# A two-layer graph network on one core: the seven-product form of A g built from four integer block sums on GpSimd and one difference on VectorE

## What is computed

```
deg = max(sum(adj != 0), 1)
x1  = layernorm(x + relu((a_norm @ x + x) @ W0 + b0))      # layer 0, a_norm = (A + I) / deg
h   = x1 @ W_sa ;  g = x1 @ W_gcnb
e   = where(A != 0, exp(-leaky_relu(s_left[i] + s_right[j], 0.01)), 0)
x_a = (e @ h) / (sum_j e + 1e-5)                           # attention part
x_b = A @ g + b_gcnb                                       # plain part, the one that changes
gate_a, gate_b = sigmoid([A x1, x1] @ Wa + ba), the same with Wb, bb
out = layernorm(x1 + sigmoid(gate_a * x_a + gate_b * x_b))
```

## Time and profile before

| what | before |
| --- | --- |
| median of 3 runs | 879.91 us (878.53 to 880.76) |
| profiled execution, from first to last instruction | 877.3 us |
| runs' median minus that span | 2.6 us |
| TensorE busy | 856.7 us (98%) |
| VectorE busy | 683.4 us (78%) |
| ScalarE busy | 571.2 us (65%) |
| GpSimd busy | 181.3 us (21%) |
| TensorE's granted clock, mean over the span | 0.996 of 2.4 GHz |

### The profile page before, as it was taken

The page is one execution under the profiler, slowest core; times in us unless marked ns, Lnnn a source line. Parts: engine busy times, 40 slices in busy tenths (PEclk is TensorE's granted clock), DMA queues, the critical chain, the costliest instruction groups (busy, mean ns, idle before and its releaser), DMA issues.

```text
span 877.3 us, 20460 instructions
## 1 busy us (share of the span) xinstructions
PE 856.7 (98%) x7579; PEld 755.0 (86%) x7579; DVE 683.4 (78%) x1182; ACT 571.2 (65%) x1214; POOL 181.3 (21%) x181
## 2 busy tenths in 40 slices
PE   8899999999999998999999999999999999999997
PEld 7787888888888887887788888888888888888886
DVE  5787676766667567898988988988978978978863
ACT  5754555555555237988977976966966967867831
POOL 1001333323322321012022022032032032032021
PEclk9999999999999999999999999999999999999999
DMA  9989999998999424110220120120120220220001
GB/s 321 305 273 320 352 401 339 360 344 315 380 316 341 174 105 144 56 55 1 79 80 15 63 78 24 54 78 15 63 78 6 71 78 0 78 78 0 25 25 37
DMA packets 66617, 130.01 MB, mean 148 GB/s; under 512 B 5464, under 2 KB 29056, under 8 KB 62080
## 3 DMA queue, kind: packets, MB, share of 16 engines
q1 hardware_dynamic: 57632, 120.87, 39.2%
q10 hardware_dynamic: 8928, 8.38, 2.8%
HBM read 99.87 MB, written 29.36 MB: 147 GB/s over the span
## 4 chain that ended last, share of the span: by engine, by line
PE 76%; issue 11%; DVE 5%; ACT 3%; DMA 3%; POOL 1%; SPq 0%; POOLq 0%; ACTq 0%; DVEq 0%
PE ps L1529 31%; PE ps L1365 21%; PE ps L1470 19%; PE ps L1400 4%; ACT ec L624 2%; DVE ec L1099 1%; DMA xs<-in_x_dram 1%; ACT em L633 1%; DMA h_scratch<-hst 1%; PE ps L1385 1%; DVE em L1106 1%; DVE dd L940 0%; POOL zb L434 0%; DMA x1r<-x_scratch 0%; SPq L335 0%
## 5 line engine op out<-in xcount | busy, mean ns | idle before, releaser
L1529 PE MATMUL ps<-fb,em 128*128 128x257 f16 x3072 | 347.5, 273 | 0.8 <-DVE em L1106 0.8
L1529 PEld LDWEIGHTS ps<-fb,em 128*128 128x128 f16 x3072 | 300.5, 98 | 38.6 <-issue 1.3
L1365 PE MATMUL ps<-y,codes 128*128 128x257 f16 x2048 | 237.8, 273 | 0.4 <-DVE y L831 0.4
L1365 PEld LDWEIGHTS ps<-y,codes 128*128 128x128 fp8e4 x2048 | 200.2, 98 | 27.0 <-DVE y L831 0.8
L624 ACT ACTIVATE ec<-slb,nsb 128x256 f32<-128x256 f32 x512 | 211.3, 499 | 0.0
L1106 DVE SCALAR_TENSOR_TENSOR em<-ec,em 128x2048 f16<-128x2048 f32 x64 | 147.4, 2303 | 22.7 <-ACT em L633 22.7
L633 ACT ACTIVATE em<-ec 128x2048 f16<-128x2048 f32 x64 | 122.1, 1910 | 65.1 <-PE ps L1529 57.0
L1099 DVE SCALAR_TENSOR_TENSOR ec<-ec,pan 128x2048 f32<-128x2048 f32 x64 | 147.3, 2302 | 2.6 <-issue 1.8
L1470 PE MATMUL ps<-zz,dd 128*128 128x256 f16 x768 | 89.4, 273 | 1.5 <-DVE t L1128 1.3
L458 POOL TENSOR_TENSOR sc<-sc,sc 128x2 f32<-128x2 f32 x15 | 38.5, 2569 | 246.3 <-DVE sc L1208 246.3
L1470 PEld LDWEIGHTS ps<-zz,dd 128*128 128x128 fp8e4 x768 | 75.0, 98 | 10.7 <-issue 2.0
(11 more groups left out here) (154 smaller groups left out, 786.0 us busy)
## 6 DMA issues: line engine op xcount, KB each, us to landing
strip<-in_adj_dram SPq DMA_DIRECT2D x128, 512.0 KB, 7.5
a_scratch<-codes SPq DMA_DIRECT2D x16, 1024.0 KB, 10.3
pan<-a_scratch SPq DMA_DIRECT2D x16, 1024.0 KB, 4.9
x_scratch<-x ACTq DMA_DIRECT2D x32, 128.0 KB, 5.3
x1r<-x_scratch SPq DMA_DIRECT2D x16, 256.0 KB, 2.8
h_scratch<-hst ACTq DMA_DIRECT2D x30, 136.0 KB, 5.5
out_dram<-ot SPq DMA_DIRECT2D x15, 256.0 KB, 2.2
fb<-h_scratch SPq DMA_DIRECT2D x3, 1088.0 KB, 8.8
```

The lines of the kernel that those rows point to most:

```text
L1365: mm = pe.matmul(ACC(n), codes[:, qq % SLOTS, h, jb, e * P:(e + 1) * P].bitcast(F8), y[:, jb, part, 0:YC], start=(jb == 0 and part == 0), ...
L1529: mm = pe.matmul(PH(2 * m + e)[:, 0:HC], em[:, c, e_part, i, e * P:(e + 1) * P], fb[:, jb, h_part, 0:HC], start=(jb == 0 and e_part + h_pa ...
```

## The change

The seven products are formed with other signs. Four of the code blocks are now sums of two blocks (x11 + x21, x21 + x22, x11 + x12, x12 + x22) and only M1's remains a difference (x11 - x22). A missing edge is now code 0 in place of 128, so that bytes add without carrying (8 + 8 = 16, which read as fp8 is 2^-5), and four codes are added at a time as one int32.

- **GpSimd** makes the four sums, `block_sum`, one int32 add of 512 words each (448 and 64 for unit 0), and signals them on a new semaphore `sum_ready`. For unit 0 the four parts of 448 words stand between the layer-0 steps of tiles 27 to 30, for unit 1 they stand ahead of `pool_bias(0)`, and in the loop the four of unit u stand ahead of `pool_bias(u-1)` and `pool_rstd(u-2)`. They wait for `prod_done` of all products of unit u - 1 and for the panel.
- **VectorE** makes only M1's block, in two instructions with a wait for its own result between them, since the sign bit must be set from the edge bit: o = x22 | (x22 << 4), then o = x11 ^ o.
- `g_sums` is five adds of 128 or 130 columns in place of three of 258, 128 and 256, since the new forms of g have mixed signs; `gb` has a fourth row. `middle_m1` subtracts and `add_67` adds where it was the other way round.
- TensorE's products, their order and their sizes stay. Its waits for four of the blocks are on `sum_ready`.

```diff
-EDGE, NONE = 8, 128
+EDGE, NONE = 8, 0
...
         def g_sums(eng, p):
             eng.wait_ge(S["g_ready"], 2 * p + 2)
-            eng.tensor_tensor(gb[:, 2, :], gb[:, 0, :], gb[:, 1, :], ALU.add)
+            eng.tensor_tensor(gb[:, 2, 0:P + 2], gb[:, 1, 0:P + 2], gb[:, 0, 0:P + 2], ALU.subtract)
+            eng.tensor_tensor(gb[:, 3, P:GC], gb[:, 0, P:GC], gb[:, 1, P:GC], ALU.subtract)
             eng.tensor_tensor(fs[:, 0, :], gb[:, 0, H1], gb[:, 1, H2], ALU.subtract)
-            eng.tensor_tensor(fs[:, 1:3, :], gb[:, 0:2, H1], gb[:, 0:2, H2], ALU.add).then_inc(S["gsum_ready"], 1)
+            eng.tensor_tensor(fs[:, 1, :], gb[:, 0, H2], gb[:, 0, H1], ALU.subtract)
+            eng.tensor_tensor(fs[:, 2, :], gb[:, 1, H1], gb[:, 1, H2], ALU.subtract).then_inc(S["gsum_ready"], 1)
...
+            def block_sum(slot, i, p0=0, p1=NP):
+                name, x, y_ = SUMS[i]
+                pool.tensor_tensor(form_of(name, p0, p1, I32), block_of(slot, x, p0, p1, I32),
+                                   block_of(slot, y_, p0, p1, I32), ALU.add).then_inc(S["sum_ready"], 1)
...
+                if T - 5 <= n < T - 1:
+                    if n == T - 5:
+                        pool.wait_ge(panel_in[0], 16)
+                    block_sum(0, n - T + 5, 0, NP - 2)
...
+            pool.wait_ge(S["r_ready"], T)
+            for i in range(NSUM):
+                block_sum(0, i, NP - 2, NP)
+            pool.wait_ge(panel_in[1], 16)
+            pool.wait_ge(S["prod_done"], 4)
+            block_sum(1, 0)
+            pool.wait_ge(S["prod_done"], NPROD + 1)
+            for i in range(1, NSUM):
+                block_sum(1, i)
             pool_bias(0)
             with pool.Fori(0, NPAN // 2 - 1) as k:
                 for i in range(2):
+                    gate(pool, panel_in[i], k * 16 + 32, "passed_pool")
+                    gate(pool, S["prod_done"], k * (2 * NPROD) + (i + 2) * NPROD, "passed_pool")
+                    for j in range(NSUM):
+                        block_sum(i, j)
                     pool_bias(k * 2 + (i + 1))
                     pool_rstd(k * 2 + i)
...
-            def difference(slot, op, p0=0, p1=NP):
-                o, a, b = differences(slot, op, p0, p1)
-                return dve.scalar_tensor_tensor(out=o, in0=b, scalar=0x7f7f7f7f, in1=a, op0=ALU.bitwise_and,
-                                                op1=ALU.bitwise_xor)
+            def difference(slot, p0=0, p1=NP):
+                o, x11, x22 = form_of("M1", p0, p1, U32), block_of(slot, X11, p0, p1, U32), block_of(slot, X22, p0, p1, U32)
+                st.then(dve.scalar_tensor_tensor(out=o, in0=x22, scalar=4, in1=x22, op0=ALU.logical_shift_left,
+                                                 op1=ALU.bitwise_or))
+                st.sync()
+                dve.tensor_tensor(o, x11, o, ALU.bitwise_xor).then_inc(S["diff_ready"], 1)
...
             middle(0)
             middle_m1(0)
-            some_differences(1, 1, DIFF_ORDER[0:2], done=4)
+            dve.wait_ge(panel_in[1], 16)
+            unit_difference(1, 1, done=4)
             mask_chunk(0, 0, 0)
...
             mask_chunk(0, 0, 1)
-            some_differences(1, 1, DIFF_ORDER[2:], done=NPROD + 1)
             middle(1)
...
             def outer_products(s, m):
                 gate(pe, S["m67_read"], s + 1, "passed_pe")
-                gate(pe, S["diff_ready"], s * NDIFF + (2 * NDIFF + 1), "passed_pe")
+                gate(pe, S["diff_ready"], s + 3, "passed_pe")
                 product(1 - m, "M1")
-                gate(pe, S["diff_ready"], s * NDIFF + (2 * NDIFF + 2), "passed_pe")
+                gate(pe, S["sum_ready"], s * NSUM + (2 * NSUM + 1), "passed_pe")
                 product(1 - m, "M6")
             def onto_products(s, m):
                 gate(pe, S["mid_read"], s * 2 + 3, "passed_pe")
-                gate(pe, S["diff_ready"], s * NDIFF + 3 * NDIFF, "passed_pe")
+                gate(pe, S["sum_ready"], s * NSUM + 3 * NSUM, "passed_pe")
```

More of the change, by code:

```diff
@@ L56 @@
 NPROD = len(PROD)
-NDIFF = 5
+NSUM = 4
 H1, H2 = slice(0, P), slice(P + 2, D + 2)
 SLOPE = 0.01
-EDGE, NONE = 8, 128
+EDGE, NONE = 8, 0
 EDGE_VAL = 2.0 ** -6
@@ L170, in build @@
     hst = area("hst", [P, 2, 2, ROW], F16)
-    gb = area("gb", [P, 3, GC], F32)
+    gb = area("gb", [P, 4, GC], F32)
     fs = area("fs", [P, 3, P], F32)
@@ L277, in g_sums, with block_of, form_of @@
             eng.wait_ge(S["g_ready"], 2 * p + 2)
-            eng.tensor_tensor(gb[:, 2, :], gb[:, 0, :], gb[:, 1, :], ALU.add)
+            eng.tensor_tensor(gb[:, 2, 0:P + 2], gb[:, 1, 0:P + 2], gb[:, 0, 0:P + 2], ALU.subtract)
+            eng.tensor_tensor(gb[:, 3, P:GC], gb[:, 0, P:GC], gb[:, 1, P:GC], ALU.subtract)
             eng.tensor_tensor(fs[:, 0, :], gb[:, 0, H1], gb[:, 1, H2], ALU.subtract)
-            eng.tensor_tensor(fs[:, 1:3, :], gb[:, 0:2, H1], gb[:, 0:2, H2], ALU.add).then_inc(S["gsum_ready"], 1)
+            eng.tensor_tensor(fs[:, 1, :], gb[:, 0, H2], gb[:, 0, H1], ALU.subtract)
+            eng.tensor_tensor(fs[:, 2, :], gb[:, 1, H1], gb[:, 1, H2], ALU.subtract).then_inc(S["gsum_ready"], 1)
         def h_place(n):
             return hst[:, n % 2] if n < T - 2 else fb[:, n]
[L286 to L296, removed]
+        X11, X21, X12, X22 = range(4)
+        FORM = {"M1": 0, "M2": 1, "M6": 2, "M5": 3, "M7": 4}
+        SUMS = (("M6", X11, X21), ("M2", X21, X22), ("M5", X11, X12), ("M7", X12, X22))
+        def block_of(slot, x, p0, p1, dt):
+            a = pan[:, slot, 2 * p0:2 * p1, :].bitcast(dt).rearrange("p (q two) c -> p q (two c)", two=2)
+            return a[:, :, x * (P // 4):(x + 1) * (P // 4)]
+        def form_of(name, p0, p1, dt):
+            return dd[:, p0:p1, 6 * P * 2:8 * ROW].bitcast(dt)[:, :, FORM[name] * (P // 4):(FORM[name] + 1) * (P // 4)]
         def gate(eng, sem, value, passed):
@@ L1047, in _ @@
                     cast(1)
[L1048 to L1053, removed]
+                if n == T - 2:
+                    dve.wait_ge(panel_in[0], 16)
+                    difference(0, 0, NP - 2)
             assert next(todo, None) is None
@@ L1065, in _ @@
             forms_lo(NP - 1)
-            for op in DIFF_ORDER:
-                difference(0, op, NP - 2, NP).then_inc(S["diff_ready"], 1)
+            difference(0, NP - 2, NP)
             def row_ends():
@@ L1107, in low_chunk, with unit_difference @@
                                          op0=ALU.mult, op1=ALU.subtract).then_inc(S["elow_ready"], 1)
-            def some_differences(u, slot, ops, done=NPROD):
+            def unit_difference(u, slot, done=NPROD):
                 gate(dve, S["prod_done"], (u - 1) * NPROD + done, "passed_dve")
-                for op in ops:
-                    difference(slot, op).then_inc(S["diff_ready"], 1)
+                difference(slot)
             def middle(u):
@@ L1125, in middle_m1 @@
                 st.sync()
-                st.then(dve.tensor_tensor(t134[:], lc[:, 2, 0:P], t134[:], ALU.add))
+                st.then(dve.tensor_tensor(t134[:], lc[:, 2, 0:P], t134[:], ALU.subtract))
                 st.sync()
@@ L1165, in add_67 @@
                 st.sync()
-                dve.tensor_tensor(wq[:, 0:4:3, :], s67[:], wq[:, 1:3, :], ALU.subtract).then_inc(S["comb_ready"], 1)
+                dve.tensor_tensor(wq[:, 0:4:3, :], s67[:], wq[:, 1:3, :], ALU.add).then_inc(S["comb_ready"], 1)
             def sums_67(u):
@@ L1251, in dve_step @@
                     sums_67(s)
-                    some_differences(s + 1, n, DIFF_ORDER)
+                    unit_difference(s + 1, n)
                 mask_chunk(s + 1, n, 1)
@@ L1298, in _ @@
             dve.wait_ge(panel_in[0], 32)
-            some_differences(2, 0, DIFF_ORDER)
+            unit_difference(2, 0)
             mask_chunk(1, 1, 3)
@@ L1303, in _ @@
             dve_step(2, 0, 2)
-            n0, per_pair = st.n, 2 * 11
+            n0, per_pair = st.n, 2 * 12
             with dve.Fori(1, NPAN // 2 - 1) as k:
@@ L1463, in product @@
                     else:
-                        d0 = 12 * P + diff[name] * P
+                        d0 = 12 * P + FORM[name] * P
                         a = dd[:, p, d0:d0 + P]
@@ L1491, in _ @@
             pe.wait_ge(S["stat_ready"], T)
-            pe.wait_ge(S["diff_ready"], 2)
+            pe.wait_ge(S["sum_ready"], 1)
             product(0, "M6", 0, early)
@@ L1496, in _ @@
             pe.wait_ge(S["g_ready"], T - 1)
-            pe.wait_ge(S["diff_ready"], NDIFF)
+            pe.wait_ge(S["sum_ready"], NSUM)
             product(0, "M2", 0, early, bank=FIRST_52[1])
```

14 lines of the change are left out of this document (6 added, 8 removed).

## The result

The changed kernel takes 885.71 us (883.93 to 887.72, 5 runs), the kernel before 880.76 in the runs beside it (878.53 to 882.47, 5 runs). The ratio is 1.0067, 95% interval 1.0045 to 1.0088: slower by 4.95 us by the medians and by 5.9 by the ratio, whose interval is 4.0 to 7.8. I had forecast 882.7, slower by 2.8, in a range of 878.5 to 891.0. The profiled execution's span is 882.1 us against 877.3.

What follows compares the result with a forecast made beforehand. TensorE was taken to bound layer 0 and the middle passes, with VectorE late in the ramp from 337 to 420 us. 0.1 + 2.1 + 0.6 = +2.8 us on 879.91 gave 882.7 us, range 878.5 to 891.0.

Steps and rivals of the forecast that it cites:

- The price h: VectorE time lost per 512-word GpSimd add when a read of two SBUF tensors comes next: taken as 1.08 us.
- VectorE becomes the bound: Rival: h near 2.16 makes VectorE's round 35.1 us, over TensorE's 33.45; 909 us, deciding from h = 1.6; chance 0.12.
- half the price: Rival: h about 0.6, or pass 0's third sum slips behind L1106; 881.0 us, within 0.3%; chance 0.26.
- Layer 0, +0.1: Layer 0: longer g_sums and unit 0's sums cost GpSimd 0, pair 15's sums on VectorE 0.1 us.
- Pass 0, +2.1: Pass 0: unit 1's sums delay chunk 0's low part by 0.3 + 0.7 + 1.1 us; TensorE's wait becomes 2.9.
- Pass 1, +0.6: Pass 1: unit 2's sums make chunk 1's low part 2.3 us later, a new wait of 1.9; net +0.6.
- Pass 2, 0: Pass 2: unit 3's sums cost 2.4 less 1.73, so 0.7 us against slack 0.8 at M2; cost 0.
- Middle passes, 0: Middle passes: VectorE's round grows by 0.7 to 31.9 us, under TensorE's 33.45; cost 0.
- Span and time: Whole kernel: the median time was taken to lie 2.6 us above the profiled span.
- The rival that the sums don't hold VectorE: Rival: integer adds leave the ports free, VectorE is 1.73 us earlier at unit 2; 878.3 us; chance 0.12.

Runs made afterwards that it cites:

- e1: The changed kernel with each GpSimd sum of units 1 to 15 adding one word in place of 512: 878.95 us, ratio 0.9975.
- e4: The changed kernel with one-word sums for units 1 to 3 only, units 4 to 15 in full: 879.01 us, ratio 0.9976.
- e2: The changed kernel with each full sum of units 1 to 15 made twice, first into a spare tile: 938.98 us, ratio 1.065.
- e5: The changed kernel with the sum blocks of units 1 to 15 made on VectorE by one bitwise or each: 882.71 us, ratio 1.0008.
- e10: The kernel before with e9's moved norm, e7's two placed bias adds and unit 2's bias add placed too: 876.23 us, ratio 0.9947.
- e9: The kernel before with pass 0's norm on ScalarE moved behind the copy lc and its high part in pass 2: 879.27 us, ratio 0.9982.
- e11: The changed kernel with e3's late sums, three bias adds placed as in e10 and e9's moved norm: 882.96 us, ratio 1.001.
- e3: The changed kernel with unit 1's last three sums held until pass 0's first low part is ready: 883.73 us, ratio 1.0028.
- e8: The changed kernel with e3's late sums and e7's two placed bias adds: 883.52 us, ratio 1.0024.
- e7: The kernel before with GpSimd's bias adds of units 0 and 1 delayed by semaphore waits: 879.75 us, ratio 0.9977.

## Why the prediction was right, and which terms were mis-sized

The mechanism and the side were right, the range held the time, and the forecast was 3.0 us under what was measured, 2.1 if the differences are compared (2.8 and 4.95), 3.1 by the ratio. "Slower" had a chance of 0.52, so the side was only just called.

- **The price h.** Taken as 1.08 from the bias add; measured 1.06 on the long instructions (3.35 for 2.29) and 1.08 on a shorter one (1.50 for 0.42), and the integer add in short runs is 1.26 us alone, where the float one is 1.27. The case "VectorE becomes the bound" needed 1.6 and "half the price" 0.6: both fell. One block takes GpSimd about twice what it takes VectorE (1.23 and 0.62 us), which by itself cost nothing. That the lock lasts a whole instruction (the Trainium skill, SBUF — State Buffer, on the two separate sides) would have given 1.27; these runs show 1.07, and 0.41 beside a copy of 0.57.
- **Layer 0, +0.1.** 0.13 between the first and the last part of unit 0's M3. Right. e1, which has the new layer 0 too, is faster than before, so layer 0 can't hide a large cost.
- **Pass 0, +2.1: measured +2.47.** M6's sum held L1143 by 0.67, not 0.3; the other two held sums 0.74 and 1.01, where I had 0.7 and 1.1. I had also missed that `fb` L959 stands behind L957 and is what M1 of unit 1 waits for, so that 1.59 us of the waiting stands there. The wait at the first chunk is 1.78, not 2.9; the two together are 3.4, and the sum is what counts.
- **Pass 1, +0.6: measured +0.78, but at another chunk.** I followed the low part of chunk 1, slack 0.4, and not that of chunk 0: in the old times it ended at 374.7 (372.49 + 2.29) for a TensorE that had been working without a stop and needed it at about 375.6 (381.01, less the wait of 1.80, less the 3.59 by which all of pass 1 begins later). With 3.7 us of sums before its end, less the 1.13 idle, 2.6 in all against a slack of 0.9, that one broke first. The net doesn't hang on which chunk waits: 2.6 less the 1.73 saved is 0.9, near the 0.78. The old 0.40 and 1.32 were taken up as forecast.
- **Pass 2, 0: measured +0.44.** "Just covered" it was not. The bias add of unit 2 fell between the two instructions of M1's block, the second took 1.65 us for 0.69, and unit 3's M1 waited 0.27. I had costed that pair as two plain instructions; it is the last thing ahead of TensorE's need. The rest of the 0.44 is not traced.
- **Middle passes, 0.** Right: 33.46 us, e4 shows it in time and e2 what lies behind the cover.
- **The rest.** These terms make 3.8 of the 4.95 us, 0.2 less than where the interval of the measurement (4.0 to 7.8) begins. 1.1 us is left by the medians, 2.1 by the ratio. The change's profiled execution, at 883.93 us, is the fastest of its five, and those five come out high against the ramp elsewhere too (e5 is 3.0 to 5 us better in time and 2.06 in the ramp, e4 6.7 to 8 and 5.37). The clock is a small part: the mean granted clock of the five is 0.9958, that of before's executions beside the experiments 0.9962 to 0.9968, by estimate 0.4 to 0.9 us (a microsecond at half speed costs half of one, and takes as much off the span times the mean clock). What the remainder is stays open.
- **Span and time.** I took 2.6 us to lie around the span. In the executions with both on record it is 1.7 to 2.2 (883.93 for 882.1 in the change); the forecast adds its 2.8 to the median and doesn't hang on it.

The rival that the sums don't hold VectorE was priced at 878.3; e1, in which they don't, gave 878.95.

## What to carry to other kernels

Work given to an idle engine is not free if its instructions hold up those of the engine that is late. Here a block costs VectorE 0.6 us if VectorE makes it and 1.07 us if GpSimd does, so moving it wins time only where the add falls into a wait of VectorE or beside its reads of PSUM, and does no harm in a stage that something else bounds. Before moving work to GpSimd, count its overlap with VectorE in the stage that waits, not in the busy share of the whole; the converse, placing GpSimd's few existing adds by a semaphore into VectorE's gaps, gained 5 us here together with one moved norm (e10; the bias adds alone 1.5 to 2.0, the norm alone 1.6 to 2.0).

## What the runs showed of the hardware that I had not expected

**The clock behind a wait.** Behind one and the same 2.07 us wait, unit 3's M3 took 5.37 us in some profiles and 3.71 in others; e1 and e4 have the same code up to there. The rows by stretch (busy PE, PEld, DVE, ACT, POOL, then the granted clock, DMA share, GB/s), before and in e1:

```profile
421.00:423.00 2.00, 2.00 (x11) 1.40 (x10) 2.00 (x2) 2.00 (x7) 0.00 (x0) 0.50 1.03 430
```
```profile
421.00:423.00 2.00, 2.00 (x20) 1.78 (x19) 2.00 (x2) 2.00 (x6) 0.00 (x0) 1.00 0.95 326
```

TensorE is at 1.2 GHz in the first (11 matmuls in 2 us) and at 2.4 in the second (20). It had worked from 409.22 to 416.41 and then stood for 2.08 us. In e9, e10 and e11, where this wait is gone, M3 took 3.71; in e11 M1 took 5.32 instead, behind the wait of 2.70. Behind the wait of 2.33 at unit 1's M2 it was 5.37 in e3 (granted clock 0.68 over it) and 3.71 in e8 and e11. What decides between the two isn't shown; DMA load alone doesn't, since its share was 0.01 in e3's stretch, at the low clock, and 0.95 in e1's, at the full one. The price is 1.66 us on top of the wait, which is why single profiles of e1 and e4 differ by 1.65 in the ramp and their medians by nothing. It also hid a wait: with M3 at 5.37 VectorE had time to catch up, with 3.71 unit 3's M2 waits 1.0 to 1.1 (e7, e9).

**Who waits for whom.** Beside VectorE's long instructions a GpSimd add takes up to two and a half times its time: 8.21 us for four sums in pass 1 and 7.74 for three in e3, against 4.93 for four at 420.38 beside VectorE's idle time and short instructions; 3.15 for a bias add, against 1.27. VectorE is held by GpSimd and GpSimd by VectorE, and that is enough to make GpSimd, idle 67% of the time, the one that TensorE waits for (2.33 us in e3, e8 and e11).
